# Queries and keys as two float32r parts in place of three bfloat16 parts, and two heads on two row tiles of the TensorE array

## The reference

```
q = x @ Wq + bq                      # 2048 x 256, split into heads
k, v = ctx @ Wk + bk, ctx @ Wv + bv  # 1601 x 256
scores = einsum('bqhd,bkhd->bhqk', q, k) / sqrt(head size)
out = einsum('bhqk,bkhd->bqhd', softmax(scores over k), v)
x = x + out @ Wo + bo
```

## Time before, and the profile's own time

| | us |
|---|---|
| median of 3 runs | 4534.62 |
| lowest and highest | 4534.21 and 4538.73 |
| span of the profiled execution | 4547.7 |
| layer 0: start to first normalization | 0 to 18.7 |
| layer 0: normalization | 18.7 to 35.2 |
| layer 0: projections, DMA of the parts, first queries | 35.2 to 114.7 |
| layer 0: prologue of maxima, turn | 114.7 to 160 |
| layer 0: the 208 steps | 160 to 809 |
| layer 2: the 208 steps | 2552 to 3175 |

### The profile page before, as it was taken

How to read it: one execution, slowest core, us unless ns; L and a number is a source line. 1 busy time by engine, 2 the same in 40 slices (tenths; PEclk the granted TensorE clock), 3 DMA queues, 4 the chain that set the end, 5 groups by cost and what they waited for, 6 DMA issues and landing times. The chain is left out here.

```text
span 4547.7 us, 61161 instructions
## 1 busy us (share of the span) xinstructions
PE 3983.5 (88%) x19174; PEld 1804.0 (40%) x19175; DVE 2670.7 (59%) x5907; ACT 1975.0 (43%) x2374; POOL 207.4 (5%) x420
## 2 busy tenths in 40 slices
PE   4999999699599999947994799999786999997894
PEld 2233333466323333335663234443441333333463
DVE  3888786445488878632224554443456887883322
ACT  2476677222247667712332243334012766765110
POOL 1000000000000000021003000000000000001202
PEclk8799999899779999958997899999795999997897
DMA  7000000000600000042113200000023000001144
GB/s 135 15 12 13 10 12 2 18 18 18 101 12 12 13 10 12 2 161 102 31 31 90 64 12 12 11 9 1 23 47 67 12 13 9 12 5 66 49 146 111
DMA packets 131231, 170.84 MB, mean 38 GB/s; under 512 B 30119, under 2 KB 111215, under 8 KB 128914
## 3 DMA queue, kind: packets, MB, share of 16 engines
q1 hardware_dynamic: 121362, 136.37, 12.2%
q0 software_dynamic: 9600, 31.04, 2.3%
HBM read 114.12 MB, written 54.66 MB: 37 GB/s over the span
## 5 line engine op out<-in xcount | busy, mean ns | idle before, releaser
L1028 DVE TENSOR_REDUCE mx<-ps 128x1 f32<-128x400 f32 (+1 forms) x3584 | 1809.8, 565 | 538.7 <-PE ps L1536 533.9
L797 ACT ACTIVATE probs<-ps,zero_col 128x1024 f32<-128x1024 f32 (+1 forms) x1040 | 1111.7, 1110 | 741.0 <-PE ps L1566 740.6
L1536 PE MATMUL ps<-k_stack,q_stack 97*128 97x400 bf16 (+3 forms) x4096 | 1233.1, 352 | 142.9 <-DMA q_stack<-ones_row 120.7
L1566 PE MATMUL ps<-q_stack,k_stack 100*128 100x512 bf16 (+2 forms) x3328 | 1080.9, 383 | 4.1 <-ACT probs L797 3.9
L1580 PE MATMUL ps<-probs,v 128*32 128x512 f32 (+2 forms) x5824 | 896.9, 611 | 0.2 <-ACT probs L797 0.2
L1536 PEld LDWEIGHTS ps<-k_stack,q_stack 97*128 97x128 bf16 (+1 forms) x4096 | 343.7, 98 | 1255.2 <-DVE mx L1028 703.6
L797 ACT ACTIVATE probs<-ps,mask_col 128x1024 f32<-128x1024 f32 (+1 forms) x416 | 440.3, 1110 | 188.1 <-PE ps L1566 187.9
L1566 PEld LDWEIGHTS ps<-q_stack,k_stack 100*128 100x128 bf16 (+2 forms) x3328 | 325.0, 100 | 321.5 <-ACT probs L797 59.1
L1283 DVE SCALAR_TENSOR_TENSOR x_res<-ps,comb,x_res 128x256 f32<-128x256 f32 x336 | 149.1, 483 | 154.5 <-PE ps L1710 154.1
L1580 PEld LDWEIGHTS ps<-probs,v 128*32 128x32 f32 (+2 forms) x5824 | 140.3, 112 | 234.1 <-issue 223.2
L1695 PE MATMUL ps<-xn_t,w_up 128*128 128x512 f32 (+1 forms) x416 | 192.8, 603 | 34.1 <-DVE comb L1182 22.6
(11 more groups left out here) (205 smaller groups left out, 2664.4 us busy)
## 6 DMA issues: line engine op xcount, KB each, us to landing
q_stack<-q_parts SPq DMA_DIRECT2D x384, 64.0 KB, 2.3
k_stack<-k_parts SPq DMA_DIRECT2D x48, 400.2 KB, 12.2
q_parts<-qk_part SPq DMA_DIRECT2D x32, 384.0 KB, 10.1
w_up<-in_up SPq DMA_DIRECT2D x17, 704.0 KB, 4.4
x_place<-zeros POOLq DMA_DIRECT2D x2, 5120.0 KB, 26.5
k_parts<-qk_part SPq DMA_DIRECT2D x24, 384.0 KB, 5.8
w_all<-in_up SPq DMA_DIRECT2D x5, 1024.0 KB, 16.4
w_all<-in_down SPq DMA_DIRECT2D x5, 1024.0 KB, 19.8
```

Of the source, the lines that this page charges most:

```text
L797: act.activation(PR[pair[0] % 4][0:r, :, :], PS[0:r, 2 * b:2 * b + 2, :], ACT.Exp, bias=mask_col[0:r, k:k + 1] if L == 3 else zero_col[0:r ...
L1028: ins = dve.reduce_max(MX4[g % 2][:, u, c:c + 1], PS[:, bank, 0:CK[c]], AX.X)
L1536: last = mm(PS[:, bank, 0:CK[c]], QS[g][0:rows, s, qt * P:(qt + 1) * P], KS[0:rows, ks0, CKO[c]:CKO[c] + CK[c]], start=sub == 0, stop=sub ...
L1566: last = mm(PS[0:r, b + i, :], KS[0:rows, (g * hpg + jj) * nsub + sub, k * P:k * P + r], QS[g][0:rows, slot_of(jj) + sub, :], start=sub == ...
```

## The change

Each value of q and k becomes the sum of two float32r parts (float32r is a 4-byte type whose writes are rounded for TensorE), and three pairs of parts are multiplied instead of six. So a head of 16 takes 48 rows plus a mask row and two rows of the negated maximum, 51 in all, and a head of 32 takes 99. Two heads of 16 stand on partitions 0 and 64 of one slot (`hps` = 2, `place_of`), and their two matmuls go to different halves of the array's rows. A head of 32 stands alone (`hps` = 1), with one matmul where there were two.

- All score and max matmuls read float32r. A max job's first chunk is 402 keys wide, one of them read twice.
- Max jobs come in pairs of heads (i = 0, 1); `side_schedule` counts pairs, so the boundary between late and early jobs moves: in layer 2 the late ones are 24 of 32 (20 before).
- In a step the side jobs are dealt before, between and after the pairs of scores; the two matmuls of a pair of scores are no longer parted by side jobs.
- DVE makes one operation per projected tile in place of three, and three per turn in place of five.
- The rows of ones and zeros are no longer loaded by DMA; POOL sets all of `k_stack` to 1 and the four `q_stack` buffers to 0 (1 in layer 3) before the projections. Layer 3 loads its mask as a row of the keys, and ACT's exponential has no bias any more; the per-partition mask and its two DMAs are gone.
- The parts in DRAM are 2 x 4 bytes a value in place of 3 x 2.

The kernel's division by PSUM sums and the 1024-wide exponential stay. The diff, cut to its core:

```diff
-CK = [401, 400, 400, 400]
+CK = [402, 400, 400, 400]
...
-ATT = [dict(dh=16, pw=32, hpg=4, nsub=1), dict(dh=16, pw=32, hpg=4, nsub=1),
-       dict(dh=32, pw=64, hpg=2, nsub=2), dict(dh=16, pw=32, hpg=4, nsub=1)]
+ATT = [dict(dh=16, pw=32, hpg=4, hps=2), dict(dh=16, pw=32, hpg=4, hps=2),
+       dict(dh=32, pw=64, hpg=2, hps=1), dict(dh=16, pw=32, hpg=4, hps=2)]
+
+Q_PART, K_PART = [0, 0, 1], [0, 1, 0]
...
-    units = hpg * TPQ
+    units = hpg // 2 * TPQ
...
     half = units * 3 // 8
-    late = [("max", (g + 1) % NG, u, c) for u in range(half, units) for c in range(4)] if nxt1 else []
-    early = [("max", (g + 2) % NG, u, c) for u in range(half) for c in range(4)] if nxt2 else []
+    late = max_jobs((g + 1) % NG, hpg, half, units) if nxt1 else []
+    early = max_jobs((g + 2) % NG, hpg, 0, half) if nxt2 else []
...
-    return [("max", g, u, c) for u in range(lo, hi) for c in range(4)]
+    return [("max", g, u, c, i) for u in range(lo, hi) for c in range(4) for i in range(2)]
...
-            KS = sb("k_stack", [100, 16, S], bf16, att)
+            KS = sb("k_stack", [P, 8, S], f32r, att)
...
+            QS = [sb(f"q_stack{i}", [P, 2, Q], f32r, att) for i in range(4)]
...
+                dh, hps = ATT[L]["dh"], ATT[L]["hps"]
+                keys = k_parts[K_PART[third]].rearrange("(s i d) n -> i d s n", i=hps, d=dh)
+                for i in range(hps):
+                    row = 64 * i + third * dh
+                    sp.dma_start(KS[row:row + dh, half * 4:half * 4 + 4, :].bitcast(f32),
+                                 keys[i][:, half * 4:half * 4 + 4, :]).then_inc(s_ks, 16)
...
+                for buf in QS:
+                    link(pool.memset(buf[:].bitcast(f32), 1.0 if L == 3 else 0.0))
+                link(pool.memset(KS[:].bitcast(f32), 1.0))
                 fence(pool, fences)
-                link(pool.memset(MP[:, 0, :], 0.0))
...
-                        act.activation(PR[pair[0] % 4][0:r, :, :], PS[0:r, 2 * b:2 * b + 2, :], ACT.Exp,
-                                       bias=mask_col[0:r, k:k + 1] if L == 3 else zero_col[0:r, :],
-                                       scale=1.0).then_inc(s_pr, 1)
-                        pair[0] += 1
+                        act.activation(PR[tile[0] % 4][0:r, :, :], PS[0:r, b:b + 2, :], ACT.Exp).then_inc(s_pr, 1)
+                        tile[0] += 1
...
-                    link(dve.tensor_tensor(r, x, p[:, 0, 0:n], ALU.subtract))
-                    link(dve.tensor_copy(p[:, 1, 0:n], r))
-                    dve.tensor_tensor(p[:, 2, 0:n], r, p[:, 1, 0:n], ALU.subtract).then_inc(s_pp, 1)
+                    dve.tensor_tensor(p[:, 1, 0:n], x, p[:, 0, 0:n].bitcast(f32), ALU.subtract).then_inc(s_pp, 1)
...
+                def place_of(j):
+                    return 64 * (j % hps), j // hps
...
+                        row, s = place_of(u // TPQ * 2 + i)
+                        end = row + 3 * dh + 1
+                        last = mm(PS[:, bank, 0:CK[c]], QS[g][row:end, s, qt * P:(qt + 1) * P],
+                                  KS[row:end, 2 * g + s, CKO[c]:CKO[c] + CK[c]], start=True, stop=True)
...
+                    for i in range(2):
+                        row, s = place_of(2 * j + i)
+                        end = row + 3 * dh + 3
+                        last = mm(PS[0:r, b + i, :], KS[row:end, 2 * g + s, k * P:k * P + r], QS[g][row:end, s, :],
+                                  start=True, stop=True)
...
-                            for job in slot[:2]:
+                            cut = chunk_of(len(slot), npair + 1)
+                            for job in slot[:cut[1]]:
                                 side(job)
-                            cut = [2 + n for n in chunk_of(max(len(slot) - 2, 0), 2 * npair)]
                             for j in range(npair):
-                                for i in range(2):
-                                    scores(g, k, j, i)
-                                    for job in slot[cut[2 * j + i]:cut[2 * j + i + 1]]:
-                                        side(job)
+                                scores(g, k, j)
+                                for job in slot[cut[j + 1]:cut[j + 2]]:
+                                    side(job)
```

184 lines of the change are left out of this document (69 added, 115 removed).

## The result

| | before | after |
|---|---|---|
| median, us | 4535.92 (4 runs) | 4698.1 (4 runs, 4686.77 to 4705.66) |
| ratio, 95% interval | | 1.0357 (1.0341 to 1.0372) |
| span of the profiled execution, us | 4547.7 | 4695.7 |
| mean granted clock | 0.915 | 0.856 |

The change made the kernel 3.6% slower. The forecast was 4424 us, 2.4% faster, with a range of 4365 to 4515; the measured time is above that range. "Steps" is from a layer's first score matmul to its last; the time at half clock is worked out from windows of 5 us, in which only the levels 1.00 and 0.50 occur but for the windows in which it changes.

The account below looks back on a forecast made before the run. Attention steps decide: four-head steps bound by PE's stream and a DVE-PE ring, layer 2 by PE. Layer 2 -112, four-head layers -15, memsets +19, projections +4, start -3, queries -3.5: -110.5 from 4534.6, 4424 us; range 4365 to 4515.

Parts of the forecast that it names:

- One cycle a column: All score and max matmuls: float32r streams one array cycle per column, as bfloat16 does, where float32 takes four.
- -172: Layer 2's matmuls: scores halve, -90 us, and max jobs lose one matmul each, -82, all on PE.
- Rival (b): float32r takes more than one cycle a column; at two cycles about 4800 us; chance 0.13.
- Layer 2's stall: Layer 2's group ends: PE waits 2.5 us for the maximum's rows at 14 of them, +35 us (25 to 45).
- The clock behind it: Layer 2: half of 14 stalls are followed by 7 us at half clock, +25 us (0 to 49).
- a sign of being wrong in kind: Layer 2: a group staying above 35 us would show the forecast wrong in kind; some 30 us was expected.
- the ring unchanged at 2.83: Four-head steps: a DVE-PE dependency loop without scores holds the step at 2.83 us; -5 a layer, -15 for three.
- Rival (a): Row tiles don't overlap and float32r weight loads cost like float32's: +75, 4500 us; chance 0.17.
- the clock unchanged at 0.99: Four-head layers: steps had a granted clock of 0.99, and the forecast gave them no term for a clock fall.
- POOL's memsets, +19: Before the projections: added memsets make POOL need 20.7 us against 16.5, fence 4.2 later, in all +19 (14 to 25).
- One sign that I named: Start of the projections: POOL's memset of k_stack ends near 39.6 and the projections begin with it.
- Projections +4, start and queries -6.5: Projections: +1 us a layer, +4 (-32 to +40); start -3 from two fewer mask DMAs; queries -3.5 from fewer issues.

Follow-up runs that it names:

- experiment 6: Changed kernel with layer 2's boundary of late and early max jobs at one half instead of three eighths, so the turn comes earlier; ratio 1.0166 to the kernel before.

## Why the prediction was wrong, point by point

- **One cycle a column**: right. Layer 2's step of three jobs is 2.20 us, and 475.5 us for its steps once the stall is gone is 140 less than before. Of the -172 some 30 are missing. By my terms that step would be 2.07; its first job takes 0.29 until the next start where I had 0.17, since its weight load is exposed behind the weighing, and I had left that out of layer 2 as I had all but left it out of the others. Rival (b) is out. (Four of 400 columns give 0.177 by the earlier trace rows, not 0.175, which makes 1 us of the sum.)
- **Layer 2's stall**: right. 31.4 us in 14 waits against +35 (25 to 45), turn to first job 4.20 us against 4.5.
- **The clock behind it**: the term that was mis-sized in layer 2. I let half of 14 stalls drop the clock for 7 us, +25 (0 to 49); it fell behind all of them, for 3 to 17 us, and cost 64 us (experiment 6). The row that I took it from, was one case at the loop's edge, and I used its length as an upper bound without reason. By this and the stall a group of layer 2 is 35.7 us (570.5/16), above the 35 that I had named as a sign of being wrong in kind; with the early turn it is 29.7, so the kind was right and the clock's term wrong.
- **Four-head layers, the ring unchanged at 2.83**: the mechanism was right, no score stands in it. The step was 2.96, because both exposed loads are longer by 0.08. I had this as 38 us a layer at most and then took 4, since a matmul seemed to start with its load; it is the next start that pays. The freed scores gave part of it back in the steps with extra work, as forecast. Taken step by step, the 489 steps of these layers that run at full clock in both kernels average 3.045 us before and 3.087 after, which for a layer is 9 us, in all 26 where -15 was forecast: off in size, within the bounds. The Trainium skill ("TensorE: Matmul & The Clock Gate", Weight-path perf modes) gives the fast load to all but FP32 and does not name float32r; the trace puts float32r with float32, as it loads 128 columns in 0.18 us (float32 0.19, bfloat16 0.098). Rival (a) had this right and the overlap wrong.
- **Four-head layers, the clock unchanged at 0.99**: the step that failed outright, since it was never written down. The forecast let the clock depend on stalls alone. Taking 49 to 51 rows in place of 97 to 100, with two tiles that overlap only in part, left the array with less to do, and 134 to 166 us a layer at half clock came of it (15 to 18 before). Of the +159 us of these layers, the 26 above are steps at full clock, so the clock is worth some 133; this is an estimate. The runs with and without doubled scores differ by less, 24 to 33 us a layer and 89 in all, because doubled scores cost time themselves: in steps at full clock 12 us a layer. No rival held this. The trace of before had a hint that I read past. In the prologue, where single max jobs wait for DVE, the clock stands at half while PE counts as busy throughout:

```profile
120.00:145.00 25.00, 25.00 (x53) 5.40 (x52) 25.00 (x53) 0.00 (x0) 0.00 (x0) 0.50 0.02 6
```

- **POOL's memsets, +19**: right engine, wrong mechanism, +50.6 measured (12.3 of it in layer 0, where I had 4.2). I costed POOL's queue against DVE's as if the two ran side by side; DVE's operation stood still for 10.9 us instead. Most of the 12.3 is the 10.5 us by which that one operation is too long. One sign that I named shows it: POOL's memsets ended 21.1 us behind their start, as I had reckoned (20.7), but the first projection began 7.7 us after them, not with them, since DVE and the transpositions had yet to follow.
- **Projections +4, start and queries -6.5**: small and roughly right: from first projection to first max job -9.6 in four layers, start -3.4, and another -8.2 in the prologues, which I had not counted (5.2 of it in layer 2, where they have half the matmuls).
- **The sum**: layer 2 came out 67 us above the forecast, the other layers 174 and the memsets 32, the rest 14 below it: -112 became -45.2, -15 became +159.4, +19 became +50.6, -2.5 became -16.8. The three large misses have one sign for a reason: the clock and DVE's run beside POOL cost nothing before, and I took both as given where the change altered what they rested on.

## What to carry to other kernels

In this kernel, packing two half-height matmuls side by side could pay only where PE's stream itself ended the step. Where a ring with another engine ended it, the packing took work from the array, and TensorE's clock went with it (0.99 to 0.88 in layer 0). So ask of each halved matmul what the array does in the freed time, and look first at stretches of the old trace in which PE counts as busy at half clock. When an operand type changes, price its weight load at every place where a matmul waits for a bank or a semaphore, since there the load was not hidden in any step read here. And a memset on POOL isn't free beside DVE: see what kind of operation DVE runs meanwhile.

## What the runs showed of the hardware

- The granted clock went with the rows of the matmuls, and not with PE's busy time alone: with 51 rows it stood at 0.50 for 100.00 us of PE's busy 100.00, with 80 or more in the same program it stayed near 1.00 but for 8 to 33 us a layer. The change came between 66 rows (284 to 387 us a layer) and 80; this is shown for this kernel only.
- The same score matmuls issued twice brought layer 0 from 166 to 23 us at half clock and the kernel from 1.036 to 1.012 of the kernel before.
- A stall of PE of 2.0 to 3.3 us was followed by a stretch at half clock, 3 to 17 us long, in all 14 cases of layer 2.
- Two float32r matmuls on different row halves started 0.01 us apart.
- A float32r weight load of 128 columns took 0.18 us at full clock, 0.28 at half; the columns of its matmuls streamed at about one cycle each (two scores and two jobs of layer 2, 1824 columns, in 0.90 us).
- A matmul of 115 rows behind one of 51 did not load its weights ahead (0.29 us each, at half clock).
- A DVE `tensor_scalar` from SBUF that met POOL's memset took 10.93 us, its median being 0.40; one on 16 columns took 4.55 in place of 0.18.
